# Attention: key blocks 5 and 6 of a pair added on VectorE over a strided view, two denominator groups on TensorE instead of three

## The chip, the core and the metric

The kernel runs on one core of a Trainium2 chip. The core has five engines that run side by side: TensorE (PE, matmuls into PSUM), VectorE (DVE), ScalarE (ACT), GpSimd (POOL) and SyncE (SP, which issues the transfers). Each takes its instructions in order and waits on semaphores for the others. The metric is the device time of one execution in microseconds: the kernel before has a median of 3039.39 us over 3 runs (3037.04 to 3043.93).

## The reference

One transformer block with adaptive layer norm over 4 sequences of 1024 tokens, width 1024, all in float32. Cut to what matters:

```python
x = L0_attn_x                                        # (4, 1024, 1024)
h = _layernorm(x) * (1 + ca) + sa                    # ca, sa, ga, ... from silu(c) @ wmod
q = (h @ wq_w + wq_b).reshape(bs, sl, 32, 32)        # 32 query heads
k = (h @ wk_w + wk_b).reshape(bs, sl, 8, 32)         # 8 key heads, 4 query heads on each
v = (h @ wv_w + wv_b).reshape(bs, sl, 8, 32)
attn = einsum('bqhfd,bkhd->bhfqk', qg, k) * scale    # scale 1/sqrt(32)
att = softmax(attn, axis=-1)
a = einsum('bhfqk,bkhd->bqhfd', att, v)
x = x + ga * (a @ wo_w + wo_b)
h = _layernorm(x) * (1 + cb) + sb
x = x + gb * lora_experts(h)                         # 4 experts of rank 16, the top 2 by router
```

The change concerns the softmax's denominator alone: for each head and query, the sum of exp over 1024 keys.

## The kernel before

Three stages follow one another: `project` (norm, modulation, q, k, v to DRAM), `attend`, `finish` (output projection, second norm, experts). The diff touches `attend` alone, which runs from about 690 to 2485 us of the span.

`attend` works through 64 pairs. A pair is two query heads of one key head over all 1024 queries: 4 chunks `c` of 512 queries each (`REP` = 4, `QW` = 512), and 8 key blocks of 128 keys. The keys lie in the partitions, so a tile of exponentials `p_t[:, s, c, :]` is 128 keys by 512 queries; `p_t` holds all 8 blocks of a pair, 4 x 512 words each per partition. One hardware loop covers 4 pairs a turn; the first and the last four pairs are written out.

TensorE goes through a pair in 8 steps (`do`, L999). Step s of a pair does, in this order:
- `add_num` (L951): values times exponentials of the block before, four matmuls 32 columns wide, one for each chunk, side by side in the array. In step 0 that is block 7 of the pair before.
- a denominator group, in steps 0, 1 and 3, for the pair before. A group is four matmuls of a 128x32 matrix of ones with 128x512, one for each chunk, into `den_ps`: they sum over the partitions. In steps 0 and 1 the right side is the exponentials of blocks 6 and 7 as they are (`add_den`, L965), in step 3 it is `p_sum` (`add_sum`, L977).
- in step 5 the turn of the next pair's maxima (`turn_max`, L928), which shares the bank of `den_ps`.
- `scores` (L939) of chunks 2 and 3 of block s into the two buffers of `st_ps`, then the first two chunks of the next block between the entries.
- two entries (`entry`, L912), two matmuls each: scores of a later pair, laid out with the queries in the partitions, into one of the two buffers of `s_ps`. Entry e waits until the maximum of entry e - 2 has been taken.

VectorE takes the maximum of every entry (`maximum`, L846, instruction L852), two a step, and in steps 4 to 7 the four pieces of the division for the pair before (`divide`, L862): transpose of `den_ps`, reciprocal, transpose back, product into `a_sb`. In step 6 it also makes `m_lo` (L859). ScalarE takes the exponentials (L832) and, in step 0, the copy of `num_ps`. GpSimd adds blocks 0 to 5 of a pair into `p_sum` in five additions of 128x2048 (L790), each after the exponentials of its block. ScalarE may overwrite a block of `p_t` only when all readers of it in the pair before are done (L822 to L826).

So of 8 blocks six are added by GpSimd and go to TensorE as one group, and two go there raw, one group each. SyncE loads q, k and v ahead and stores `a_sb`; the change leaves its program as it is.

Of the kernel before, what the change touches and what calls it, by code (L numbers as in the profile page):

```python
# [5 lines left out]
ALU = mybir.AluOpType  # L6
ACT = mybir.ActivationFunctionType
F32 = mybir.dt.float32
# [4 lines left out]
P = 128  # L13
# [4 lines left out]
def is_int(i, value):  # L18

    return isinstance(i, int) and i == value  # L20
# [566 lines left out]
def attend(nc, w_o, ident, wo_hi, wo_lo, q_hi_d, q_lo_d, k_hi_d, k_lo_d, v_d, att_d):  # L587
# [16 lines left out]
    ROWS = STACK + 2  # L604
    QR = 4
    NS = HEADS * NKT
    SUMMED = 6
    SUMS = SUMMED - 1
    RAWS = NKT - SUMMED
    SUM_STEP = 3  # L610
    TURN_STEP = 5
    FIRST = 18
    assert KT == NKT and NS == 16 and RAWS == 2


    START_PLAN = [(1, e) for e in range(FIRST - NS, NS)] + [(2, e) for e in range(NS // 2)]
# [3 lines left out]
    def below(i, value):  # L620
        return isinstance(i, int) and i < value
# [11 lines left out]
    with ExitStack() as ctx:  # L633
        def sb(name, shape, dt):
            return ctx.enter_context(nc.sbuf_tensor(name, shape, dt))
# [4 lines left out]
        def sem(name):  # L640
            return ctx.enter_context(nc.semaphore(name))
# [3 lines left out]
        v_sb = sb("v_sb", [P, 2, NKT, HD], F32)  # L645
        p_t = sb("p_t", [P, NKT, REP, QW], F32)
        p_sum = sb("p_sum", [P, 2, REP, QW], F32)
        ones = sb("ones", [P, HD], F32)
        mx = sb("mx", [P, 2, NS], F32)
        m_hi = sb("m_hi", [NS, P], F32R)  # L650
# [25 lines left out]
        st_ready = sem("st_ready")  # L676
        exp_done = sem("exp_done")
        num_done = sem("num_done")
        den_done = sem("den_done")
        sum_done = sem("sum_done")  # L680
        sum_used = sem("sum_used")
        num_taken = sem("num_taken")
        den_taken = sem("den_taken")
        rden_step = sem("rden_step")
# [3 lines left out]
        def pairs(eng, do):  # L688

            for pair in range(QR):  # L690
                do(pair, pair, pair // 2)
            with eng.Fori(1, NPAIR // QR - 1) as n:
                for slot in range(QR):
                    do(n * QR + slot, slot, n * 2 + slot // 2)
            for pair in range(NPAIR - QR, NPAIR):
                do(pair, pair % QR, pair // 2)

        with nc.Block() as block:
# [70 lines left out]
            @block.gpsimd  # L769
            def _(pool):  # L770
                nc.gpsimd.memset(ones[:, :], 1.0).then_inc(consts, 1)

                for k in range(KT):
                    pool.wait_ge(wo_hi_done, k + 1)
                    nc.gpsimd.tensor_tensor(wo_lo[:, k, :], p_t[:, k, 0:D // QW, :].rearrange("p j n -> p (j n)"),
                                            wo_hi[:, k, :].bitcast(F32), ALU.subtract).then_inc(wo_lo_done, 1)

                def do(pair, slot, it):
                    total = p_sum[:, slot % 2, :, :]
                    for kt in range(1, SUMMED):  # L780
                        pool.wait_ge(exp_done, pair * TILES + (kt * REP + REP))
                        if kt == 1:
                            if not below(pair, 2):

                                pool.wait_ge(sum_used, pair - 1)
                            before = p_t[:, 0, :, :]
                        else:
                            pool.wait_ge(sum_done, pair * SUMS + (kt - 1))
                            before = total
                        nc.gpsimd.tensor_tensor(total, before, p_t[:, kt, :, :], ALU.add).then_inc(sum_done, 1)  # L790

                pairs(pool, do)

            @block.scalar
            def _(act):
                for k in range(KT):
                    act.wait_ge(wo_in[k // (KT // 2)], 16)
                    nc.scalar.copy(wo_hi[:, k, :], p_t[:, k, 0:D // QW, :].rearrange("p j n -> p (j n)"))\
                      .then_inc(wo_hi_done, 1)

                def max_hi(pair):

                    act.wait_ge(m_turned, pair + 1)
                    if not is_int(pair, 0):
                        act.wait_ge(m_in, pair * 32)
                    nc.scalar.activation(m_hi[:, :], m_ps, ACT.Copy, scale=-1.0).then_inc(m_hi_done, 1)

                def take_num(pair):
                    act.wait_ge(num_done, pair * STEPS + STEPS)
                    if not below(pair, 1):  # L810

                        act.wait_ge(a_ready, pair)
                    nc.scalar.copy(num_sb[:, :], num_ps[:, :]).then_inc(num_taken, 1)

                max_hi(0)

                def do(pair, slot, it):
                    for s in range(STEPS):
                        if not below(pair, 1):


                            act.wait_ge(num_done, (pair - 1) * STEPS + (s + 1))  # L822
                            if s < SUMMED:
                                act.wait_ge(sum_done, (pair - 1) * SUMS + max(s, 1))
                            else:
                                act.wait_ge(den_done, (pair - 1) * RAWS + (s - SUMMED + 1))  # L826
                        else:

                            act.wait_ge(wo_lo_done, s + 1)
                        for c in range(REP):  # L830
                            act.wait_ge(st_ready, pair * TILES + (s * REP + c + 1))
                            nc.scalar.activation(p_t[:, s, c, :], st_ps[:, c % 2, :], ACT.Exp, scale=SCALE)\  # L832
                              .then_inc(exp_done, 1)
                            if c == 1 and s == 0 and not below(pair, 1):
                                take_num(pair - 1)
                            if c == 1 and s == TURN_STEP and not is_int(pair, NPAIR - 1):
                                max_hi(pair + 1)

                pairs(act, do)
                take_num(NPAIR - 1)  # L840

            @block.vector
            def _(dve):
# [11 lines left out]
                def max_lo(pair):  # L855
                    dve.wait_ge(m_hi_done, pair + 1)
                    if not is_int(pair, 0):
                        dve.wait_ge(m_in, pair * 32)
                    nc.vector.scalar_tensor_tensor(m_lo[:, :], m_ps, -1.0, m_hi[:, :].bitcast(F32), ALU.mult,  # L859
                                                   ALU.subtract).then_inc(m_lo_done, 1)  # L860

                def divide(pair, par, piece):  # L862


                    if piece == 0:
                        dve.wait_ge(sum_used, pair + 1)
                        nc.vector.transpose(den_t[:, :, :].rearrange("p c r -> p (c r)"), den_ps[:, :])\
                          .then_inc(den_taken, 1)
                    elif piece == 1:
# [25 lines left out]
                def do(pair, slot, it):  # L895
                    for s in range(STEPS):
                        if s == TURN_STEP + 1 and not is_int(pair, NPAIR - 1):
                            max_lo(pair + 1)
                        if s > SUM_STEP and not below(pair, 1):
                            divide(pair - 1, (slot - 1) % 2, s - SUM_STEP - 1)  # L900
                        for item in beside(pair, slot, s):
                            maximum(*item)

                pairs(dve, do)
                for piece in range(4):
                    divide(NPAIR - 1, (NPAIR - 1) % 2, piece)

            @block.tensor
            def _(pe):
# [52 lines left out]
                                                p_t[:, s, c, :], start=s == 0, stop=s == NKT - 1)  # L962
                    last.then_inc(num_done, 1)

                def add_den(pair, s):  # L965

                    if s == SUMMED:
                        if below(pair, 1):
                            pe.wait_ge(m_lo_done, 2)
                        else:  # L970
                            pe.wait_ge(a_ready, pair)
                    for c in range(REP):
                        last = nc.tensor.matmul(den_ps[c * HD:(c + 1) * HD, :], ones[:, :], p_t[:, s, c, :],
                                                start=s == SUMMED, stop=False)
                    last.then_inc(den_done, 1)

                def add_sum(pair, par):  # L977

                    pe.wait_ge(sum_done, pair * SUMS + SUMS)
                    for c in range(REP):  # L980
                        last = nc.tensor.matmul(den_ps[c * HD:(c + 1) * HD, :], ones[:, :], p_sum[:, par, c, :],
                                                start=False, stop=True)
                    last.then_inc(sum_used, 1)

                def entries(pair, part):
                    for e in part:
# [12 lines left out]
                def do(pair, slot, it):  # L999
                    for s in range(STEPS):  # L1000
# [2 lines left out]
                        before = (pair, slot, s - 1) if s else (pair - 1, (slot - 1) % QR, STEPS - 1)  # L1003
                        if not (below(pair, 1) and s == 0):
                            add_num(*before)
                        if s < RAWS and not below(pair, 1):
                            add_den(pair - 1, SUMMED + s)
                        if s == SUM_STEP and not below(pair, 1):
                            add_sum(pair - 1, (slot - 1) % 2)
                        if s == TURN_STEP and not is_int(pair, NPAIR - 1):  # L1010
                            turn_max(pair + 1, (slot + 1) % QR)

# [17 lines left out]
                    scores(0, 0, 0, c)  # L1030
                pairs(pe, do)
                add_num(NPAIR - 1, QR - 1, STEPS - 1)
                for s in range(SUMMED, NKT):
                    add_den(NPAIR - 1, s)
                add_sum(NPAIR - 1, (NPAIR - 1) % 2)


def finish(nc, x, b_o, lora_in, lora_out, earlier_in, ident, wo_hi, wo_lo, att_d, mod_raw_d, mod_gate_d, out):
# [504 lines left out]
```

## Time and profile before

| | before |
|---|---|
| median of 3 runs | 3039.39 us |
| lowest, highest | 3037.04, 3043.93 us |
| profiled execution, its own time | 3039.35 us |
| its span, first to last instruction | 3037.6 us |
| TensorE busy in the span | 2899.8 us (95%) |
| VectorE busy | 1930.1 us (64%) |
| GpSimd busy | 1799.0 us (59%) |
| ScalarE busy | 1525.5 us (50%) |
| mean granted clock of TensorE | 0.975 |

A busy share over the whole span averages three stages with different limits, so it has to be read by stage. Within a stage the timeline tells more than the sums: it gives the start of each instruction, and what ended the idle time before it in brackets. Matmuls are pipelined: the next starts before the last has ended, so the distance between two starts is the price of one, not its duration. The same holds on VectorE for instructions that wait for nothing. Of two merged instructions ("x2") the row gives the start of the first and the time to the end of the last.

### The profile page before, as it was taken

How to read it: one execution, taken by the hardware profiler on the slowest of the kernel's cores; microseconds unless marked ns; L12 is line 12 of the kernel's file. 1: busy time of each engine (PE TensorE's matmuls, PEld its weight loads, DVE VectorE, ACT ScalarE, POOL GpSimd, SP SyncE). 2: the span in 40 equal slices, each digit the busy share in tenths (PEclk: the TensorE clock that was granted, in tenths of full speed). 3: DMA queues.
4: the chain of work that ended last, by engine and by line, in shares of the span. 5: the costliest groups of instructions: out<-in, count | busy, mean ns of one | idle time of the engine just before them, and what ended most of it. 6: DMA issues, size and time to landing. Idle time of an engine off the chain costs nothing. (4 is left out here: it accounts for less than half of the span.)

```text
span 3037.6 us, 49792 instructions
## 1 busy us (share of the span) xinstructions
PE 2899.8 (95%) x15590; PEld 1743.7 (57%) x15590; DVE 1930.1 (64%) x2572; ACT 1525.5 (50%) x2906; POOL 1799.0 (59%) x595
## 2 busy tenths in 40 slices
PE   6899999989999999999999999999999978999997
PEld 3687878864444444444444444444444427777776
DVE  3333333327777777777777777777777717666666
ACT  2211111115666666666666666666666643444444
POOL 2433333317888888888888888888888865111110
PEclk7899999988999999999999999999999989999998
DMA  6543333341222122212211221122122123322331
GB/s 228 171 139 131 132 132 132 120 149 41 55 52 53 38 51 55 48 39 54 51 43 47 51 55 39 47 55 51 36 54 51 29 83 109 105 92 95 104 104 63
DMA packets 156463, 241.61 MB, mean 80 GB/s; under 512 B 48993, under 2 KB 90401, under 8 KB 156321
## 3 DMA queue, kind: packets, MB, share of 16 engines
q1 hardware_dynamic: 156320, 240.05, 27.3%
q8 instruction: 48, 0.79, 0.1%
q14 instruction: 95, 0.77, 0.1%
HBM read 159.12 MB, written 79.82 MB: 79 GB/s over the span
## 5 line engine op out<-in xcount | busy, mean ns | idle before, releaser
L852 DVE TENSOR_REDUCE mx<-s_ps 128x1 f32<-128x1024 f32 x1024 | 1203.5, 1216 | 430.3 <-PE s_ps L921 424.4
L832 ACT ACTIVATE p_t<-st_ps 128x512 f32<-128x512 f32 x2048 | 1112.6, 595 | 552.9 <-PE st_ps L947 483.9
L790 POOL TENSOR_TENSOR p_sum<-p_sum,p_t 128x2048 f32<-128x2048 f32 x256 | 1173.8, 4585 | 22.1
L947 PE MATMUL st_ps<-q_st,k_st 98*128 98x512 f32 x2048 | 811.2, 436 | 10.7 <-ACT p_t L832 7.7
L947 PEld LDWEIGHTS st_ps<-q_st,k_st 98*128 98x128 f32 x2048 | 345.1, 187 | 604.8 <-ACT p_t L832 414.2
L921 PE MATMUL s_ps<-k_st,q_st 96*128 96x512 f32 x2048 | 655.9, 402 | 14.5 <-DMA q_st<-q_hi_d 10.8
L961 PE MATMUL num_ps<-p_t,v_sb 128*32 128x512 f32 x4096 | 546.4, 605 | 0.9 <-ACT p_t L832 0.9
L790 POOL TENSOR_TENSOR p_sum<-p_t 128x2048 f32<-128x2048 f32 x64 | 293.3, 4584 | 293.8 <-ACT p_t L832 293.8
L921 PEld LDWEIGHTS s_ps<-k_st,q_st 96*128 96x128 f32 x2048 | 389.6, 191 | 93.7 <-DVE mx L852 14.1
L372 POOL TENSOR_TENSOR o_lo<-side,o_hi 128x512 fp32r<-128x512 f32 x80 | 104.6, 1308 | 345.1 <-ACT o_hi L342 345.1
L1231 POOL TENSOR_TENSOR a_lo<-a_f,a_hi 128x1024 fp32r<-128x1024 f32 x32 | 76.2, 2380 | 390.3 <-ACT a_hi L1266 390.2
L557 PE MATMUL o_ps<-h_hi,w_hi 128*128 128x512 f32 x608 | 243.1, 400 | 2.5 <-issue 2.4
L557 PE MATMUL o_ps<-h_hi,w_lo 128*128 128x512 f32 x608 | 239.6, 394 | 0.0
L557 PE MATMUL o_ps<-h_lo,w_hi 128*128 128x512 f32 x608 | 239.4, 394 | 0.0
L461 DVE TENSOR_SCALAR side<-o_ps,bias_qk 128x512 f32<-128x512 f32 x80 | 59.9, 749 | 277.5 <-PE o_ps L557 275.0
L342 ACT CAST o_hi<-side 128x512 fp32r<-128x512 f32 x80 | 49.7, 621 | 356.0 <-DVE side L461 344.6
L1425 PE MATMUL o_ps<-wo_hi,a_hi 128*128 128x512 f32 x512 | 205.9, 402 | 13.8 <-POOL a_lo L1231 13.8
L1425 PE MATMUL o_ps<-wo_lo,a_hi 128*128 128x512 f32 x512 | 205.2, 401 | 0.0
L1425 PE MATMUL o_ps<-wo_hi,a_lo 128*128 128x512 f32 x512 | 205.0, 400 | 0.0
L1282 ACT ACTIVATE h_t<-t_ps,shift,scale 128x128 f32<-128x128 f32 x256 | 92.8, 468 | 195.0 <-PE t_ps L1488 195.0
L961 PEld LDWEIGHTS num_ps<-p_t,v_sb 128*32 128x32 f32 x4096 | 80.6, 108 | 129.5 <-issue 125.6
L363 POOL TENSOR_TENSOR h_lo<-h_f,h_hi 128x256 fp32r<-128x256 f32 x128 | 91.6, 737 | 100.7 <-ACT h_hi L335 100.7
(129 smaller groups left out, 2819.3 us busy)
## 6 DMA issues: line engine op xcount, KB each, us to landing
q_st<-q_hi_d SPq DMA_DIRECT2D x128, 256.0 KB, 4.5
stage<-w_mod SPq DMA_DIRECT2D x48, 512.0 KB, 5.7
q_hi_d<-o_hi SPq DMA_DIRECT2D x64, 256.0 KB, 2.0
q_lo_d<-o_lo SPq DMA_DIRECT2D x64, 256.0 KB, 2.0
q_st<-q_lo_d SPq DMA_DIRECT2D x64, 256.0 KB, 4.1
att_d<-a_sb SPq DMA_DIRECT2D x128, 128.0 KB, 2.3
a_f<-att_d SPq DMA_DIRECT2D x32, 512.0 KB, 4.7
x_sb<-x SPq DMA_DIRECT2D x32, 512.0 KB, 5.3
```

The lines of the kernel that those rows point to most:

```text
L363: nc.gpsimd.tensor_tensor(h_lo[:, 1 - par, kt, cols], h_f[:, bank_at(i, hf, kt), :], h_hi[:, 1 - par, kt, cols].bitcast(F32), ALU.subtract)\
L372: nc.gpsimd.tensor_tensor(o_lo[:, g % 2, :], o_f[:, g % 2, :], o_hi[:, g % 2, :].bitcast(F32), ALU.subtract)\
L557: last = nc.tensor.matmul(o_ps[:, bank, :], w[:, kt, g * P:(g + 1) * P], h[:, par, kt, :], start=begin, stop=end)
L790: nc.gpsimd.tensor_tensor(total, before, p_t[:, kt, :, :], ALU.add).then_inc(sum_done, 1)
L832: nc.scalar.activation(p_t[:, s, c, :], st_ps[:, c % 2, :], ACT.Exp, scale=SCALE)\
L852: nc.vector.tensor_reduce(mx[:, slot % 2, e:e + 1], s_ps[:, e % 2, :], AX_X, ALU.max)\
L921: part = nc.tensor.matmul(s_ps[:, e % 2, n * QW:(n + 1) * QW], q_st[0:STACK, slot, jj, t * P:(t + 1) * P], k_st[0:STACK, slot // 2, n * QW ...
L947: nc.tensor.matmul(st_ps[:, c % 2, :], k_st[:, slot // 2, s * P:(s + 1) * P], q_st[:, slot, jj, h * QW:(h + 1) * QW], start=True, stop=True)\
L961: last = nc.tensor.matmul(num_ps[c * HD:(c + 1) * HD, :], v_sb[:, slot // 2, s, :], p_t[:, s, c, :], start=s == 0, stop=s == NKT - 1)
L1231: nc.gpsimd.tensor_tensor(a_lo[:, u, :, :], a_f[:, u, :, :], a_hi[:, u, :, :].bitcast(F32), ALU.subtract).then_inc(a_lo_done, 1)
L1282: last = nc.scalar.activation(h_t[:, tt % 2, kt, :], t_ps[:, kt * P:(kt + 1) * P], ACT.Identity, bias=batch(shift2, bb)[:, kt:kt + 1], sca ...
L1425: last = nc.tensor.matmul(o_ps[:, u, cols], a[:, u, k, :], w[:, k, cols], start=(k == 0 and n == 0), stop=(k == KT - 1 and n == 2))
```

## The change

GpSimd now adds blocks 0 to 4 and 7 (`ADDED`), again in five additions; the last one follows the exponentials of block 7. Blocks 5 and 6 are added by VectorE: for each chunk c one `tensor_reduce` with add over `p_t[:, 5:7, c, :]`, seen with the block as the innermost dimension, so that every output is the sum of two words that lie 4 x 512 words (8 KB) apart in the partition. It writes 512 words of a new buffer `two_sum`. Chunk 0 is done in step 7 of the pair itself, chunks 1 to 3 in steps 0, 1 and 2 of the next, each time ahead of that step's two maxima. TensorE now has two denominator groups a pair: over `p_sum` in step 2 and over `two_sum` in step 3; `add_den` is gone. ScalarE waits for the last reduction before it overwrites blocks 5 and 6.

```diff
-    SUMMED = 6
-    SUMS = SUMMED - 1
-    RAWS = NKT - SUMMED
-    SUM_STEP = 3
+    ADDED = (0, 1, 2, 3, 4, 7)
+    SUMS = len(ADDED) - 1
+    TWO = 5
+    SUM_STEP = 2
+    TWO_STEP = 3
...
+        two_sum = sb("two_sum", [P, REP, QW], F32)
...
-                            if s < SUMMED:
-                                act.wait_ge(sum_done, (pair - 1) * SUMS + max(s, 1))
+                            if s in ADDED:
+                                act.wait_ge(sum_done, (pair - 1) * SUMS + max(ADDED.index(s), 1))
                             else:
-                                act.wait_ge(den_done, (pair - 1) * RAWS + (s - SUMMED + 1))
+                                act.wait_ge(two_done, (pair - 1) * REP + REP)
...
+                def add_two(pair, c):
+
+                    dve.wait_ge(exp_done, pair * TILES + ((TWO + 1) * REP + c + 1))
+                    if c == 0 and not below(pair, 1):
+                        dve.wait_ge(two_used, pair)
+                    nc.vector.tensor_reduce(two_sum[:, c, :], p_t[:, TWO:TWO + 2, c, :].rearrange("p s q -> p q s"),
+                                            AX_X, ALU.add).then_inc(two_done, 1)
...
-                        if s > SUM_STEP and not below(pair, 1):
-                            divide(pair - 1, (slot - 1) % 2, s - SUM_STEP - 1)
+                        if s > TWO_STEP and not below(pair, 1):
+                            divide(pair - 1, (slot - 1) % 2, s - TWO_STEP - 1)
+                        if s < REP - 1 and not below(pair, 1):
+                            add_two(pair - 1, s + 1)
+                        if s == STEPS - 1:
+                            add_two(pair, 0)
                         for item in beside(pair, slot, s):
                             maximum(*item)
...
+                def add_two(pair):
+
+                    pe.wait_ge(two_done, pair * REP + REP)
+                    for c in range(REP):
+                        last = nc.tensor.matmul(den_ps[c * HD:(c + 1) * HD, :], ones[:, :], two_sum[:, c, :],
                                                 start=False, stop=True)
-                    last.then_inc(sum_used, 1)
+                    last.then_inc(two_used, 1)
...
-                        if s < RAWS and not below(pair, 1):
-                            add_den(pair - 1, SUMMED + s)
                         if s == SUM_STEP and not below(pair, 1):
                             add_sum(pair - 1, (slot - 1) % 2)
+                        if s == TWO_STEP and not below(pair, 1):
+                            add_two(pair - 1)
```

The queue of VectorE before, where pair 2 ends and pair 3 begins: from the maxima of step 6 and the product `a_sb` of step 7 to the division of step 4 and 5 (`mx` are the maxima, `den_t` and `rden_c` pieces of the division).

```order
L852 TENSOR_REDUCE mx<-s_ps 128x1 x2
L885 TENSOR_TENSOR a_sb<-den_ps,num_sb 128x512
L852 TENSOR_REDUCE mx<-s_ps 128x1 x10
L867 STREAM_TRANSPOSE den_t<-den_ps 128x512
L852 TENSOR_REDUCE mx<-s_ps 128x1 x2
L871 RECIPROCAL rden_c<-den_t 128x16
```

The same place now: from the maxima of step 6 of pair 2 to the transpose in step 4 of pair 3 (`two_sum<-p_t` is the new reduction).

```order
L855 TENSOR_REDUCE mx<-s_ps 128x1 x2
L896 TENSOR_TENSOR a_sb<-den_ps,num_sb 128x512
L870 TENSOR_REDUCE two_sum<-p_t 128x512
L855 TENSOR_REDUCE mx<-s_ps 128x1 x2
L870 TENSOR_REDUCE two_sum<-p_t 128x512
L855 TENSOR_REDUCE mx<-s_ps 128x1 x2
L870 TENSOR_REDUCE two_sum<-p_t 128x512
L855 TENSOR_REDUCE mx<-s_ps 128x1 x2
L870 TENSOR_REDUCE two_sum<-p_t 128x512
L855 TENSOR_REDUCE mx<-s_ps 128x1 x4
L878 STREAM_TRANSPOSE den_t<-den_ps 128x512
```

The ten maxima in a row between `a_sb` and `den_t` now have four reductions among them, one ahead of each of the first four steps' maxima (steps 7, 0, 1, 2).

The queue of TensorE before, steps 0 and 1 of pair 3 (`num_ps` are the values, `den_ps` the denominator, `st_ps` and `s_ps` the two kinds of scores).

```order
L961 MATMUL num_ps<-p_t,v_sb 32x512 x4
L973 MATMUL den_ps<-p_t,ones 32x512 x4
L947 MATMUL st_ps<-q_st,k_st 128x512 x2
L921 MATMUL s_ps<-k_st,q_st 128x512 x3
L947 MATMUL st_ps<-q_st,k_st 128x512
L921 MATMUL s_ps<-k_st,q_st 128x512
L947 MATMUL st_ps<-q_st,k_st 128x512
L961 MATMUL num_ps<-p_t,v_sb 32x512 x4
L973 MATMUL den_ps<-p_t,ones 32x512 x4
L947 MATMUL st_ps<-q_st,k_st 128x512 x2
```

TensorE now, from step 1 of pair 3 to the start of step 2.

```order
L978 MATMUL num_ps<-p_t,v_sb 32x512 x4
L964 MATMUL st_ps<-q_st,k_st 128x512 x2
L938 MATMUL s_ps<-k_st,q_st 128x512 x3
L964 MATMUL st_ps<-q_st,k_st 128x512
L938 MATMUL s_ps<-k_st,q_st 128x512
L964 MATMUL st_ps<-q_st,k_st 128x512
L978 MATMUL num_ps<-p_t,v_sb 32x512 x4
L990 MATMUL den_ps<-p_sum,ones 32x512 x4
L964 MATMUL st_ps<-q_st,k_st 128x512 x2
```

Step 1 has no denominator group any more (nor has step 0), and step 2 has the one over `p_sum`; the one over `two_sum` follows in step 3.

## Rows read from the trace of the kernel before

**Rows 1.** Page, part 2: busy tenths in 40 slices of the span.
```profile
PE   6899999989999999999999999999999978999997
...
DVE  3333333327777777777777777777777717666666
```

**Rows 2.** Busy time in one stretch: PE, PEld, DVE, ACT, POOL, clock, DMA.
```profile
1400.00:2400.00 1000.00, 998.79 (x5555) 469.40 (x5557) 757.10 (x758) 656.15 (x1228) 826.03 (x181) 1.00 0.20 48
```

**Rows 3.** Timeline, TensorE: start us, us, engine, line, what, count.
```profile
1502.34 1.07 PE L961 MATMUL num_ps<-p_t,v_sb 128*32 128x512 f32 x8
...
1503.34 0.73 PE L947 MATMUL st_ps<-q_st,k_st 98*128 98x512 f32 x2
...
1506.43 0.72 PE L947 MATMUL st_ps<-q_st,k_st 98*128 98x512 f32 x2
...
1508.60 1.07 PE L961 MATMUL num_ps<-p_t,v_sb 128*32 128x512 f32 x8
...
1510.45 0.73 PE L947 MATMUL st_ps<-q_st,k_st 98*128 98x512 f32 x2
...
1514.41 0.73 PE L947 MATMUL st_ps<-q_st,k_st 98*128 98x512 f32 x2
...
1517.50 0.72 PE L947 MATMUL st_ps<-q_st,k_st 98*128 98x512 f32 x2
...
1518.07 0.85 PE L921 MATMUL s_ps<-k_st,q_st 96*128 96x512 f32 x3
...
1518.75 0.43 PE L947 MATMUL st_ps<-q_st,k_st 98*128 98x512 f32 x1
...
1529.95 0.64 PE L961 MATMUL num_ps<-p_t,v_sb 128*32 128x512 f32 x4
```

**Rows 4.** One line's instructions, L806: durations ns, first and last start us.
```profile
L806 ACT ACTIVATE m_hi<-den_ps x64: 266/267/268, 692.7 to 2442.7; 16x128 fp32r<-16x128 f32 x64
```

**Rows 5.** Timeline, VectorE, same stretch.
```profile
1504.76 2.32 DVE L852 TENSOR_REDUCE mx<-s_ps 128x1 f32<-128x1024 f32 x2
1507.00 0.67 DVE L885 TENSOR_TENSOR a_sb<-den_ps,num_sb 128x512 f32<-128x512 f32 x1
1507.66 2.36 DVE L852 TENSOR_REDUCE mx<-s_ps 128x1 f32<-128x1024 f32 x2
...
1518.72 2.36 DVE L852 TENSOR_REDUCE mx<-s_ps 128x1 f32<-128x1024 f32 x2 [0.72 <-PE s_ps L921]
```

**Rows 6.** Groups of instructions: busy us, mean ns, idle us before them.
```profile
L852 DVE TENSOR_REDUCE mx<-s_ps 128x1 f32<-128x1024 f32 x1024 | 1203.5, 1216 | 430.3 <-PE s_ps L921 424.4
L790 POOL TENSOR_TENSOR p_sum<-p_sum,p_t 128x2048 f32<-128x2048 f32 x256 | 1173.8, 4585 | 22.1
```

**Rows 7.** Timeline of pair 0, VectorE and TensorE.
```profile
711.34 3.49 DVE L852 TENSOR_REDUCE mx<-s_ps 128x1 f32<-128x1024 f32 x3 [0.67 <-PE s_ps L921]
...
711.63 0.39 PE L921 MATMUL s_ps<-k_st,q_st 96*128 96x512 f32 x1
...
712.62 0.73 PE L921 MATMUL s_ps<-k_st,q_st 96*128 96x512 f32 x2 [0.33 <-DVE mx L852]
```

**Rows 8.** Groups of VectorE, shapes apart: copies, reductions, a two-input operation.
```profile
L1324 DVE TENSOR_TENSOR x<-x,x_sb 128x1024 f32<-128x1024 f32 x32 | 41.4, 1293 | 1.1
...
L1381 DVE TENSOR_REDUCE rank<-above 128x4 f32<-128x16 f32 x32 | 5.4, 169 | 1.1
...
L1389 DVE TENSOR_REDUCE total<-wts 128x1 f32<-128x4 f32 x32 | 5.0, 157 | 1.1
...
L1305 DVE COPY shift<-t_ps 128x32 f32<-128x32 f32 x1 | 0.2, 192 | 16.3 <-PE t_ps L1458 16.3
...
L429 DVE COPY shift<-t_ps 128x32 f32<-128x32 f32 x1 | 0.2, 191 | 1.2 <-PE t_ps L531 1.2
```

**Rows 9.** Timeline, end of the last pair.
```profile
2472.50 9.23 POOL L790 TENSOR_TENSOR p_sum<-p_sum,p_t 128x2048 f32<-128x2048 f32 x2
...
2481.78 1.06 PE L981 MATMUL den_ps<-p_sum,ones 128*32 128x512 f32 x8 [1.16 <-POOL p_sum L790]
```

More of the change, by code:

```diff
@@ L606, in attend @@
     NS = HEADS * NKT
-    SUMMED = 6
-    SUMS = SUMMED - 1
-    RAWS = NKT - SUMMED
-    SUM_STEP = 3
+    ADDED = (0, 1, 2, 3, 4, 7)
[3 more added lines that the diff above has]
+    TWO_STEP = 3
     TURN_STEP = 5
     FIRST = 18
-    assert KT == NKT and NS == 16 and RAWS == 2
+    assert KT == NKT and NS == 16 and sorted(ADDED + (TWO, TWO + 1)) == list(range(NKT))
     START_PLAN = [(1, e) for e in range(FIRST - NS, NS)] + [(2, e) for e in range(NS // 2)]
@@ L678, in attend @@
         num_done = sem("num_done")
-        den_done = sem("den_done")
         sum_done = sem("sum_done")
         sum_used = sem("sum_used")
+        two_done = sem("two_done")
+        two_used = sem("two_used")
         num_taken = sem("num_taken")
@@ L779, in do @@
                     total = p_sum[:, slot % 2, :, :]
-                    for kt in range(1, SUMMED):
+                    for n, kt in enumerate(ADDED[1:]):
                         pool.wait_ge(exp_done, pair * TILES + (kt * REP + REP))
-                        if kt == 1:
+                        if n == 0:
                             if not below(pair, 2):
                                 pool.wait_ge(sum_used, pair - 1)
-                            before = p_t[:, 0, :, :]
+                            before = p_t[:, ADDED[0], :, :]
                         else:
-                            pool.wait_ge(sum_done, pair * SUMS + (kt - 1))
+                            pool.wait_ge(sum_done, pair * SUMS + n)
                             before = total
@@ L860, in max_lo @@
                                                    ALU.subtract).then_inc(m_lo_done, 1)
+                def add_two(pair, c):
[4 more added lines that the diff above has]
+                                            AX_X, ALU.add).then_inc(two_done, 1)
                 def divide(pair, par, piece):
                     if piece == 0:
-                        dve.wait_ge(sum_used, pair + 1)
+                        dve.wait_ge(two_used, pair + 1)
                         nc.vector.transpose(den_t[:, :, :].rearrange("p c r -> p (c r)"), den_ps[:, :])\
@@ L904, in _ @@
                 pairs(dve, do)
+                for c in range(1, REP):
+                    add_two(NPAIR - 1, c)
                 for piece in range(4):
@@ L963, in add_num @@
                     last.then_inc(num_done, 1)
[L965 to L975, printed above, removed]
                 def add_sum(pair, par):
                     pe.wait_ge(sum_done, pair * SUMS + SUMS)
+                    if below(pair, 1):
+                        pe.wait_ge(m_lo_done, 2)
+                    else:
+                        pe.wait_ge(a_ready, pair)
                     for c in range(REP):
                         last = nc.tensor.matmul(den_ps[c * HD:(c + 1) * HD, :], ones[:, :], p_sum[:, par, c, :],
+                                                start=True, stop=False)
+                    last.then_inc(sum_used, 1)
+                def add_two(pair):
+                    pe.wait_ge(two_done, pair * REP + REP)
+                    for c in range(REP):
+                        last = nc.tensor.matmul(den_ps[c * HD:(c + 1) * HD, :], ones[:, :], two_sum[:, c, :],
                                                 start=False, stop=True)
-                    last.then_inc(sum_used, 1)
+                    last.then_inc(two_used, 1)
                 def entries(pair, part):
@@ L1032, in _ @@
                 add_num(NPAIR - 1, QR - 1, STEPS - 1)
-                for s in range(SUMMED, NKT):
-                    add_den(NPAIR - 1, s)
                 add_sum(NPAIR - 1, (NPAIR - 1) % 2)
+                add_two(NPAIR - 1)
 def finish(nc, x, b_o, lora_in, lora_out, earlier_in, ident, wo_hi, wo_lo, att_d, mod_raw_d, mod_gate_d, out):
```

## The prediction

> **What bounds the kernel now.** I read the page's slices first: the middle of the run, from about 690 to 2440 us, has TensorE at nine tenths or more of every slice, VectorE at seven [rows 1]. The summed stretch of that middle says it exactly: TensorE is busy 998.79 of 1000 us at a granted clock of 1.00, VectorE 757, GpSimd 826 [rows 2]. The change lies only in this attention stage, so I then read the stage as a sequence. Blocks below are the eight key blocks of a pair, steps the eight passes of the loop in `do`, and the start of a step is taken where its first pair of `st_ps` matmuls starts.
>
> An ordinary step takes 3.10 us: 1503.34 to 1506.43 [rows 3]. A step with a denominator group takes 3.96 (1510.45 to 1514.41). A whole pair takes 27.61 us (1502.34 to 1529.95 for the same `num_ps` group) and the mean over the 63 distances between 64 pairs is (2442.7 - 692.7) / 63 = 27.78 [rows 3, 4]; the difference is the turn of the hardware loop every fourth pair. TensorE never waits in there, so anything taken from its queue is time, as long as nobody else becomes late.
>
> Who could is VectorE. Its 16 maxima a pair read `s_ps`, which has two buffers. In the step that starts at 1517.50 the first entry matmul starts 0.57 later; three entries are 1518.75 - 1518.07 = 0.68 us, so 0.23 each, and the third starts 1.03 after the step's start. The first maximum starts at 1518.72, 1.22 after it, and two take 2.36 [rows 3, 5]. With 1.22 for one [rows 6], the second starts 1.14 behind the first. The third entry of a step may start when the second maximum of the step before has ended. The handover is seen where it does bind: three maxima from 711.34 end the first at 712.56, and TensorE's entry starts at 712.62, 0.06 later; its two matmuls then take 0.73, where two at the usual spacing take 0.23 + 0.39 = 0.62, so a broken stream costs 0.11 more [rows 6, 7]. I call the distance from a step's start to its first maximum the lag. TensorE waits when lag + 2.36 + 0.06 is over step + 1.03, for an ordinary step when the lag is over 1.71. The largest lag now is 1.42, in step 6 (1504.76 - 1503.34), and 1.23 in step 7 [rows 3, 5]. Nothing waits.
>
> **The change, part by part.** Removed from TensorE: one of three denominator groups a pair. Its price is 3.96 - 3.10 = 0.86 us, and 64 of them are 55 us. The other two groups move from steps 0, 1 and 3 to steps 2 and 3; the order of the queue shows this, and their cost is unchanged.
>
> Added to VectorE: four reductions a pair, each 128x1024 in and 128x512 out, ahead of the two maxima in steps 7, 0, 1 and 2. No row shows such an operation. The nearest rows: the maximum over as many elements, from PSUM, has 1.22 and a spacing of 1.14 [rows 5, 6]. Writing more outputs seems free: a reduction of 16 to 4 takes 169 ns, one of 4 to 1 takes 157, so 12 more elements read and three more written are 12 ns [rows 8]. The far view is the open point, since neighbours in the inner direction lie 8 KB apart. The only pair of rows on a far step is a copy of 32 elements out of PSUM with a step of 8 elements, 191 ns, and one without a step, 192 ns [rows 8]: no price there, though it is PSUM and short. Bounds: from below 0.67 us, a 128x512 operation (`a_sb`, 1507.00 to 1507.66) [rows 5], if only outputs counted; from above 2.28, twice the spacing of the maximum, if every hop cost one more element's time; the two-input operation of 1024 elements in SBUF, 1.29 [rows 8], lies between. I take 1.14, the row of the same operation and size.
>
> One rule speaks against this. The Trainium skill, "Vector Engine (DVE) Microarchitecture Reference", section 5.2, says that a port streams at full rate only over runs of two adjacent words, and gives 1.73 ns per column for one source that hops at every element. By it a reduction has some 1.8 us, an estimate from that page. The same section adds that a one-source operation whose stream alternates between two regions 16 KiB apart, writing one word for two read, ran at the full rate, which is nearly this view. No row here shows either; the sum goes by the maximum's row, and the slow one is a rival.
>
> Now the chain. After step 6 VectorE no longer has idle time. From the start of step 6: its first maximum 1.42 later. To that of step 7: two maxima 2.28, the product `a_sb` 0.66 and one reduction 1.14, together 4.08, where the step has 3.10: the lag becomes 2.4, over 1.71, and TensorE waits in step 0. To the first maximum of step 0: 2.28 + 1.14 = 3.42. The third entry of step 1 waits for that step's second maximum: 2.36 + 0.06. From there to the next step 3.10 - 1.03 = 2.07, with 0.11 for the restart, and the group now in step 2, 0.86. Sum from step 6 to step 2: 1.42 + 4.08 + 3.42 + 2.42 + 2.07 + 0.11 + 0.86 = 14.38 us. Before it is 1517.50 - 1503.34 = 14.16 [rows 3]. So the pair does not get shorter by 0.86; it gets 0.22 longer. The waits in steps 0 and 1 take about 1.1 us. In step 2 the long step lets VectorE catch up: the third entry is free 0.4 after its start and due at 1.03. Steps 3 to 6 are as before.
>
> 63 distances by 0.22 are +14 us. Against it: the loop's turn, 27.78 - 27.61 = 0.17 a pair, partly falls into the wait in step 0 since the chain there is VectorE's; I give it half, -5. In the last pair there is no entry to wait for; its sums end on GpSimd, at 2481.73, and TensorE waited for them [rows 9]. Two groups fewer stand ahead of its first sum (-1.7), and one more group stands behind the last (+0.9): -0.8. Sum: +8 us on the profiled execution's own 3039.35, 3047. That execution stands at the median of 3039.39, so nothing is to be corrected.
>
> What I cost at nothing. GpSimd's fifth sum is now over block 7 and not 5. The `num_ps` group of that block starts at 1508.60, so its exponentials are done by then [rows 3]; 4.59 later [rows 6] is 1513.2. Step 2 starts at 1517.50 now, its `num_ps` group 1.00 before; less the two groups that went ahead of it and plus that `num_ps` group's 0.86, its denominator group comes at 1516.5 - 1.7 + 0.9 = 1515.7 at the earliest: 2.5 us to spare. GpSimd has 5 x 4.59 = 22.9 us a pair of 27. ScalarE's wait for blocks 5 and 6 is for reductions made three steps earlier. TensorE's group over `two_sum` follows the last reduction by more than a microsecond. If the first cover went, each us would be 63.
>
> **Rivals.** First, the hop is paid. Place: the same chain, one or two steps longer. For a spacing y it is 15.80 + 4y from step 6 to step 4 (1.42 + 2.94 + 3 x 2.28 + 4y + 2.42 + 2.07 + 0.11), against 14.16 + 3.96 + 3.10 = 21.22 before. At 2.28 that is 24.9, +3.7 a pair, some 3270 us; the load of VectorE itself, 0.757 x 27.6 + 4 x 2.28 = 30.0 a pair, is over 27.6 as well. Halfway, at 1.71, it is 22.6, +1.4 and some 3128. For it: no row has two neighbours so far apart. Against it: the copy with a step. By the Trainium skill's 1.73 ns per column (same page and section), an estimate, the sum would be some 3155.
>
> Second, on the other side: faster. The two reductions in the chain (steps 7 and 0) decide twice: from step 6 to 2 the chain is 12.10 + 2y, equal to 14.16 at y = 1.03. Below that TensorE's group comes back. At the lower bound of 0.67 the chain gives 13.44, 0.72 less a pair, 2993 us. At 0.95, or if the handover is looser than 0.06 and the restart is not paid, 3026 to 3034. For it: a result only every second element. Against: 1.14 for the same count of inputs.
>
> Third, the change does nothing to the order of the work: excluded by the queues, which have the reductions and one group less.
>
> **How the numbers follow.** Forecast 0.64: 3047, own range 3034 to 3062, from 0.1 us either way on the spacing (two reductions, 63 pairs: 13 us). The hop paid 0.19, the cheaper chain 0.17. The range goes down to 3026 and up to 3165, which leaves out the doubled reduction and the cheapest. A change of 0.2%, 6 us, is about what a measurement of this kernel can tell from none. Within the forecast: slower 0.39, same 0.23, faster 0.02; with the rivals (0.19 slower; 0.15 faster and 0.02 same) slower 0.58, same 0.25, faster 0.17.
>
> **What would show it.** The reduction's mean duration near 1.2 us; VectorE without idle time from step 6 to step 2; TensorE's entries idle on `mx`, about 1 us a pair in two steps, where there is none now; steps 3 to 6 unchanged at 3.10 and 3.96; TensorE's busy share of the stage down from 99.9% to about 97% at clock 1.00; a pair of 27.8 us. Wrong it would be with a reduction of 1.8 us or more, or of 1.0 or less, or with a wait of TensorE on `p_sum`.

## The result, and the profile after

| | before | after |
|---|---|---|
| median | 3038.52 us (20 runs) | 3044.82 us (20 runs) |
| lowest, highest | 3030.67, 3045.82 | 3040.46, 3050.40 |
| profiled execution | 3039.35 us | 3043.16 us |

The ratio of the runs is 1.0022, with a 95% interval of 1.0013 to 1.0031: 4 to 9 us slower. Forecast was 8 us slower. A denominator group of TensorE is gone from each of 64 pairs, and the kernel is no faster.

The page's slices show first where it went: VectorE, at seven tenths before [rows 1], is at nine.

```profile
PE   6899999989999999999999999999999968999997
...
DVE  3333333328999999999998999999899937666666
```

In the same stretch as [rows 2], TensorE is busy 979.33 us where it had 998.79, at the same clock of 1.00, and VectorE 909.53 where it had 757.10. TensorE has less to do and about 2% of idle time.

```profile
1400.00:2400.00 1000.00, 979.33 (x5252) 458.03 (x5244) 909.53 (x899) 650.82 (x1224) 823.13 (x181) 1.00 0.20 48
```

The new group of VectorE, with busy time, mean and idle time: 1240 ns a reduction, 24 more than the 1216 of a maximum before [rows 6].

```profile
L855 DVE TENSOR_REDUCE mx<-s_ps 128x1 f32<-128x1024 f32 x1024 | 1200.4, 1212 | 167.2 <-PE s_ps L938 159.3
...
L870 DVE TENSOR_REDUCE two_sum<-p_t 128x512 f32<-128x1024 f32 x256 | 316.9, 1240 | 6.2 <-ACT p_t L835 6.2
```

Waits from 800 to 2400 us: in total, times, the longest. There was none of these in the steady state before.

```profile
PEld s_ps L938 <- DVE mx L855: 58.4, 90, 0.8
...
PE s_ps L938 <- DVE mx L855: 15.9, 44, 0.4
```

The timeline of TensorE, to be read against [rows 3]. A pair takes 1528.56 - 1500.87 = 27.69 us, where it took 27.61. An entry is two matmuls here, and the "third entry" of a step is the third of its four entry matmuls, the first that needs the second maximum of the step before. The bracket at 1509.68 is the wait for that maximum, at the third entry of step 0.

```profile
1500.87 1.06 PE L978 MATMUL num_ps<-p_t,v_sb 128*32 128x512 f32 x8
...
1501.87 0.73 PE L964 MATMUL st_ps<-q_st,k_st 98*128 98x512 f32 x2
...
1504.96 0.73 PE L964 MATMUL st_ps<-q_st,k_st 98*128 98x512 f32 x2
...
1508.12 0.73 PE L964 MATMUL st_ps<-q_st,k_st 98*128 98x512 f32 x2
...
1509.68 0.50 PE L938 MATMUL s_ps<-k_st,q_st 96*128 96x512 f32 x1 [0.38 <-DVE mx L855]
...
1511.80 0.73 PE L964 MATMUL st_ps<-q_st,k_st 98*128 98x512 f32 x2
...
1516.10 0.74 PE L964 MATMUL st_ps<-q_st,k_st 98*128 98x512 f32 x2
...
1528.56 1.06 PE L978 MATMUL num_ps<-p_t,v_sb 128*32 128x512 f32 x8
```

VectorE in the same stretch, to be read against [rows 5]. From the maxima of step 6 (1503.29) to the last reduction (1516.39) it has no idle time.

```profile
1503.29 2.32 DVE L855 TENSOR_REDUCE mx<-s_ps 128x1 f32<-128x1024 f32 x2
1505.53 0.68 DVE L896 TENSOR_TENSOR a_sb<-den_ps,num_sb 128x512 f32<-128x512 f32 x1
1506.12 1.24 DVE L870 TENSOR_REDUCE two_sum<-p_t 128x512 f32<-128x1024 f32 x1
1507.28 2.34 DVE L855 TENSOR_REDUCE mx<-s_ps 128x1 f32<-128x1024 f32 x2
1509.55 1.24 DVE L870 TENSOR_REDUCE two_sum<-p_t 128x512 f32<-128x1024 f32 x1
1510.70 2.34 DVE L855 TENSOR_REDUCE mx<-s_ps 128x1 f32<-128x1024 f32 x2
1512.97 1.24 DVE L870 TENSOR_REDUCE two_sum<-p_t 128x512 f32<-128x1024 f32 x1
1514.13 2.33 DVE L855 TENSOR_REDUCE mx<-s_ps 128x1 f32<-128x1024 f32 x2
1516.39 1.25 DVE L870 TENSOR_REDUCE two_sum<-p_t 128x512 f32<-128x1024 f32 x1
```

The lag is 1503.29 - 1501.87 = 1.42 in step 6 (forecast 1.42), 1507.28 - 1504.96 = 2.32 in step 7 (forecast 2.4), and the first maximum of step 0 follows 3.42 later, at 1510.70 (forecast 3.42). The third entry of step 0 starts at 1509.68: two maxima end at 1507.28 + 2.34 = 1509.62, and the handover is 0.06. From step 6 to step 2 it is 1516.10 - 1501.87 = 14.23 us, where it was 14.16 and 14.38 was forecast. Step 0 takes 1511.80 - 1508.12 = 3.68 us and step 1 4.30; without waits, in experiment 4, they take 3.18 and 3.97. So the waits take 0.83 us a pair, where about 1.1 was forecast.

Over all pairs, by the line of `m_hi` as in [rows 4]: (2445.0 - 691.1) / 63 = 27.84 where it was 27.78.

```profile
L809 ACT ACTIVATE m_hi<-den_ps x64: 266/266/268, 691.1 to 2445.0; 16x128 fp32r<-16x128 f32 x64
```

### The profile page after: what moved, and what is told of

The parts are those of the page before. It is cut to its first block and busy times, and to the rows that moved or that the text cites. A ratio compares the mean times of both kernels' runs of the same rounds, so it can differ in the third digit from the quotient of the medians.

```text
span 3041.4 us, 49431 instructions
## 1 busy us (share of the span) xinstructions
PE 2867.3 (94%) x15078; PEld 1723.5 (57%) x15078; DVE 2207.6 (73%) x2828; ACT 1520.6 (50%) x2906; POOL 1797.6 (59%) x595
## 5 line engine op out<-in xcount | busy, mean ns | idle before, releaser
L938 PE MATMUL s_ps<-k_st,q_st 96*128 96x512 f32 x2048 | 682.1, 407 | 36.7 <-DVE mx L855 21.2
L870 DVE TENSOR_REDUCE two_sum<-p_t 128x512 f32<-128x1024 f32 x256 | 316.9, 1240 | 6.2 <-ACT p_t L835 6.2
```

What stands on the lines that cost most here:

```text
L870: nc.vector.tensor_reduce(two_sum[:, c, :], p_t[:, TWO:TWO + 2, c, :].rearrange("p s q -> p q s"), AX_X, ALU.add).then_inc(two_done, 1)
L938: part = nc.tensor.matmul(s_ps[:, e % 2, n * QW:(n + 1) * QW], q_st[0:STACK, slot, jj, t * P:(t + 1) * P], k_st[0:STACK, slot // 2, n * QW ...
```

## The experiments

Each kernel ran beside the kernel before on the same chip. Ratios are to it, with the 95% interval.

**1. No reductions.** The waits for them stay, as plain increments:

```diff
-                    nc.vector.tensor_reduce(two_sum[:, c, :], p_t[:, TWO:TWO + 2, c, :].rearrange("p s q -> p q s"),
-                                            AX_X, ALU.add).then_inc(two_done, 1)
+                    dve.sem_inc(two_done, 1)
```

> The changed kernel without VectorE's reductions: `two_sum` is filled with ones once, so the sums of blocks 5 and 6 are left out. Theory A (the removed denominator group is worth its 0.86 us a pair, and late maxima behind the reductions take it back): no wait of TensorE on mx, 64 x 0.86 = 55 us less than before, some 2984 us. Theory B (the group was worth less, because TensorE's step has another limit): clearly above 3000 us.

Measured: 3009.32 us against 3042.12, ratio 0.9887 (0.9865 to 0.9908), 33 us less. From 800 to 2400 us of its trace TensorE's entries wait for a maximum once, 0.3 us. So the reductions take back what the group gives, but the group gives 33 and not 55. Theory A is right on who, and too high on how much. The time is above 3000, as theory B had it, and B is right that a step of TensorE has another limit in places: experiment 4 shows that it is ScalarE.

**2. The reductions alone,** in the kernel before, at the same places, with its three groups:

```diff
+                        if s < REP - 1 and not below(pair, 1):
+                            add_two(pair - 1, s + 1)
+                        if s == STEPS - 1:
+                            add_two(pair, 0)
```

> The kernel before with the four reductions a pair added at the places of the change, and the three denominator groups left as they were, in steps 0, 1 and 3; the reductions' result is not used. Theory A: the long steps 0 and 1 of before leave room. Lag 2.3 in step 7 against a limit of 2.6 ahead of a step of 4.02, 1.7 in step 0 against 2.6, 1.2 in step 1, 1.6 in step 2: no wait, within 3 us of before. Theory C (the reductions cost by themselves: reads that slow other engines, or VectorE's load): 3045 us or more, and longer additions of GpSimd or exponentials.

Measured: 3039.71 us against 3042.12, ratio 0.9996 (0.9984 to 1.0008). 256 reductions of 1.24 us cost nothing where the steps are long, and no entry waits for a maximum from 800 to 2400 us. GpSimd's addition takes 4585 ns as before [rows 6] and an exponential 595. That excludes contention and the bare load as a cause (theory C).

**3. Without the reduction in step 7,** and its counterpart **5, without the one in step 2.** Both take one of four from VectorE:

```diff
+                    if c == 0:
+                        dve.sem_inc(two_done, 1)
+                        return
```

(with `c == 3` in experiment 5).

> The changed kernel without the reduction of chunk 0, the one in step 7; its part of `two_sum` is ones, so blocks 5 and 6 are left out for that chunk. Theory A: the lag is 1.2 in step 7, 1.5 in step 0 and 1.8 in step 1, under the limits of 1.7, 1.7 and 2.6: no wait at all, some 2985 us, as without any reduction. Theory C (what counts is VectorE's load): a quarter of the difference between all four and none, some 3030 us.

> The changed kernel without the reduction of chunk 3, the one in step 2; its part of `two_sum` is ones. The counterpart to dropping the one in step 7: the same load is taken off VectorE. Theory A: step 2's reduction lies behind the last entry that waits, so nothing changes, 3044 us. Theory C (load): some 3030 us, as for any one of the four.

Measured: without the one in step 7, 3002.94 us, ratio 0.9871 (0.9852 to 0.9889). Without the one in step 2, 3045.90 us, ratio 1.0019 (1.0004 to 1.0033), as slow as with all four. The waits for a maximum, from 800 to 2400 us, first without step 7's, then without step 2's:

```profile
PEld s_ps L942 <- DVE mx L856: 0.5, 2, 0.3
```

```profile
PEld s_ps L942 <- DVE mx L856: 59.6, 92, 0.8
...
PE s_ps L942 <- DVE mx L856: 16.3, 45, 0.4
```

The first is 0.5 us in two waits, the second the same 59.6 as with all four (58.4). The same load taken off, all of the price in one case and none in the other: what counts is the chain from step 6 to the third entry of step 1, not VectorE's busy share. The first time lies 18 us above the 2985 that was expected, for the reason that experiment 4 shows.

**4. Each reduction one step later,** in steps 0 to 3, and TensorE's group over `two_sum`, which has to follow the last of them, ahead of the `num_ps` group of step 4:

```diff
-                        if s < REP - 1 and not below(pair, 1):
-                            add_two(pair - 1, s + 1)
-                        if s == STEPS - 1:
-                            add_two(pair, 0)
+                        if s < REP and not below(pair, 1):
+                            add_two(pair - 1, s)
...
+                        if s == TWO_STEP + 1 and not below(pair, 1):
+                            add_two(pair - 1)
                         if not (below(pair, 1) and s == 0):
                             add_num(*before)
```

> All four reductions, each one step later (steps 0, 1, 2, 3), and TensorE's group over two_sum behind step 3 instead of in it, ahead of the num_ps group of step 4. The same work on every engine. Theory A: lags of 1.2, 1.5, 1.8, 1.3 and 1.6 in steps 7 to 3, none over its limit (1.7, 1.7, 2.6, 1.7, 2.6): some 2985 us, 1.8% under before. Theory C (load or contention): no change against the changed kernel, 3044 us.

Measured: 3005.33 us against 3042.12, ratio 0.9876 (0.9859 to 0.9894): the same instructions on every engine, and 1.2% faster than before, where the changed kernel is 0.2% slower. It beats both kernels. It lies 20 us above the expected 2985, and its trace tells why. The starts of `m_hi`, one a pair:

```profile
1024.32 0.27 ACT L809 ACTIVATE m_hi<-den_ps 16x128 fp32r<-16x128 f32 x1 [0.68 <-PE den_ps L951]
...
1052.39 0.27 ACT L809 ACTIVATE m_hi<-den_ps 16x128 fp32r<-16x128 f32 x1 [0.68 <-PE den_ps L951]
...
1079.23 0.27 ACT L809 ACTIVATE m_hi<-den_ps 16x128 fp32r<-16x128 f32 x1 [0.68 <-PE den_ps L951]
...
1106.08 0.27 ACT L809 ACTIVATE m_hi<-den_ps 16x128 fp32r<-16x128 f32 x1 [0.68 <-PE den_ps L951]
```

The first distance is a pair behind a turn of the hardware loop, 28.07 us; the other two are 26.84 and 26.85. Before, the same were 28.06 and 27.62 (from its trace). So the missing group gives 0.77 in an ordinary pair and nothing in each fourth; over all 13 pairs behind a turn the mean is 28.12 before and 28.13 here. Without waits the pair is the same in experiments 1 and 3: 26.85.

The 0.77 instead of 0.86: step 0 takes 1090.59 - 1087.40 = 3.19 without a group, not 3.10. ScalarE copies `num_ps` in it, between the exponentials (timeline):

```profile
1087.40 1.07 PE L976 MATMUL num_ps<-p_t,v_sb 128*32 128x512 f32 x8
...
1088.53 0.58 ACT L816 COPY num_sb<-num_ps 128x512 f32<-128x512 f32 x1 [0.42 <-PE num_ps L976]
...
1090.59 1.06 PE L976 MATMUL num_ps<-p_t,v_sb 128*32 128x512 f32 x8
```

The nothing: ScalarE comes late behind its branch. At a turn its first exponential starts 1.39 after the `num_ps` group, and TensorE waits for it with its scores until 1469.44:

```profile
1467.40 1.06 PE L976 MATMUL num_ps<-p_t,v_sb 128*32 128x512 f32 x8
...
1468.79 1.08 ACT L835 ACTIVATE p_t<-st_ps 128x512 f32<-128x512 f32 x2 [1.93 <-PE num_ps L976]
...
1469.44 0.98 PE L962 MATMUL st_ps<-q_st,k_st 98*128 98x512 f32 x2 [0.97 <-ACT p_t L835]
```

The bracket names `num_ps`, but the exponential does not use that group: at the turn shown in experiment 8 the same exponential starts 2.4 us ahead of it, after a pause of 2.27 us. In the kernel before, the same pause is there, 2.17 us of ScalarE, and a denominator group stood in it:

```profile
1480.27 1.07 PE L961 MATMUL num_ps<-p_t,v_sb 128*32 128x512 f32 x8
...
1481.15 1.04 PE L973 MATMUL den_ps<-p_t,ones 128*32 128x512 f32 x8
...
1481.90 1.08 ACT L832 ACTIVATE p_t<-st_ps 128x512 f32<-128x512 f32 x2 [2.17 <-PE num_ps L961]
```

The loop's 14 passes have 13 such turns. So 13 of 64 groups had been hidden all along; 51 x 0.77 = 39 us is what the group was worth, and 37 were measured.

**6. The view.** The same 1024 words in and 512 out, of adjacent words:

```diff
-                    nc.vector.tensor_reduce(two_sum[:, c, :], p_t[:, TWO:TWO + 2, c, :].rearrange("p s q -> p q s"),
+                    nc.vector.tensor_reduce(two_sum[:, c, :], p_t[:, TWO + c // 2, c % 2 * 2:c % 2 * 2 + 2, :]
+                                            .rearrange("p c (q w) -> p (c q) w", w=2),
```

> The changed kernel with the reductions over adjacent words: each adds neighbouring queries of block 5 or 6, the same 1024 words in and 512 out, so the blocks' sums are mixed up among queries. If the view over 8 KB costs nothing: the same 1.24 us and 3044 us. If it costs part of the 25 ns that the reduction has over the maximum: 1.21 us, and 3041 us.

Measured: 1206 ns, 34 less than over the far view, and 3044.80 us against 3040.62, ratio 1.0019 (1.0008 to 1.0029). The far view costs 34 ns of 1240. The duration came out as in the second case expected, the time as in the first. In the trace an ordinary pair takes 27.60 us, 0.08 less than with the far view (27.68), as two reductions in the chain would have it; those 5 us do not show between the two ratios, 1.0019 and 1.0022.

```profile
L870 DVE TENSOR_REDUCE two_sum<-p_t 128x512 f32<-128x1024 f32 x256 | 308.2, 1206 | 6.2 <-ACT p_t L835 6.2
```

**7. Hops that reach no neighbour,** queries 16 apart and the two blocks innermost:

```diff
+                    nc.vector.tensor_reduce(junk[:, c % 2, :].rearrange("p (b a) -> p b a", b=16),
+                                            p_t[:, TWO:TWO + 2, c, :].rearrange("p s (a b) -> p b a s", b=16),
+                                            AX_X, ALU.add).then_inc(two_done, 1)
```

> The changed kernel with the reduction's view walked so that both streams jump: queries 0, 16, 32 and so on, the two blocks innermost, so that no two reads in 32 fall on neighbouring words; written to a spare buffer, with two_sum left at ones. Theory D (full rate comes from the two alternating streams each walking adjacent words): the reduction gets slower, 1.7 to 2.6 us, as by the section on the access granule in the Trainium skill's page Vector Engine (DVE) Microarchitecture Reference, and the kernel 3130 to 3330 us. Theory E (a hop is free for a one-input operation): 1.24 us and 3044 us.

Measured: 2025 ns, and 3168.78 us against 3040.62, ratio 1.0422 (1.0404 to 1.0439). Theory D holds.

```profile
L874 DVE TENSOR_REDUCE junk<-p_t 128x512 f32<-128x1024 f32 x256 | 518.0, 2025 | 6.2 <-ACT p_t L836 6.2
```

A pair takes 1110.07 - 1080.32 = 29.75 us:

```profile
1080.32 0.27 ACT L810 ACTIVATE m_hi<-den_ps 16x128 fp32r<-16x128 f32 x1 [0.68 <-PE den_ps L958]
...
1110.07 0.27 ACT L810 ACTIVATE m_hi<-den_ps 16x128 fp32r<-16x128 f32 x1 [0.67 <-PE den_ps L958]
```

The prediction's chain for this rival, 15.80 + 4y at a spacing of 2025 less the 0.08 by which a follower starts early, y = 1.94, gives 23.56, 2.34 over the 21.22 of before, a pair of 29.95. That rival was well priced; its condition did not arise.

**8, 9 and 10. The turn of the loop.** The later placement with 8 and with 28 pairs in a turn, and the kernel before with 8:

```diff
-            with eng.Fori(1, NPAIR // QR - 1) as n:
-                for slot in range(QR):
-                    do(n * QR + slot, slot, n * 2 + slot // 2)
+            with eng.Fori(0, (NPAIR - 2 * QR) // 8) as n:
+                for j in range(8):
+                    do(n * 8 + (QR + j), j % QR, n * 4 + (QR + j) // 2)
```

> The later placement with 8 pairs in a turn of the hardware loop instead of 4: 7 turns, not 14, nothing else changed. A pair behind a turn takes 28.1 us there against 26.85, since ScalarE has its first exponentials about 2 us late after its branch. Theory A (that is why the removed group gave 0.77 us in an ordinary pair and nothing at a turn): 7 x 1.2 = 8 us under the 3005 of the later placement, some 2997 us. Theory F (the cost lies in loading code, by length and not by turn): no gain, 3005 us or more.

> The kernel before with 8 pairs in a turn of the loop. Its pair behind a turn takes 28.1 against 27.62, since the denominator group of step 0 runs in ScalarE's pause. Theory A: 7 x 0.45 = 3 us under before, 3037 us. Theory F: no gain or slower.

> The later placement with 28 pairs in a turn: 2 turns instead of 14. Theory A: 12 x 1.2 = 15 us under the 3005 of the later placement, some 2990 us, near the 55 us of 64 groups. Theory F: longer straight code brings the same pauses elsewhere, 3000 us or more.

Measured: 3033.59 us, ratio 0.9977 (0.9966 to 0.9989), where 4 pairs in a turn gave 0.9876; the kernel before 3073.71, ratio 1.0112 (1.0095 to 1.0130); 28 pairs 3001.48, ratio 0.9877 (0.9857 to 0.9898). My expectations of 2997, 3037 and 2990 were all too low, and theory F is nearer. Where the loop of 8 no longer turns, the cost is gone: the pairs half way through its body take 26.85, so it belongs to the turn and not to every fourth pair. But a turn of 8 pairs is dearer than two of 4: a pair behind it takes 1047.53 - 1012.95 = 34.58 us, and the six turns 32.1 to 35.2, 33.7 in the mean. The one turn of the 28-pair loop costs as much, 33.44, so from 8 pairs on the price did not grow with the body.

```profile
1012.95 0.27 ACT L809 ACTIVATE m_hi<-den_ps 16x128 fp32r<-16x128 f32 x1 [0.68 <-PE den_ps L951]
...
1047.53 0.27 ACT L809 ACTIVATE m_hi<-den_ps 16x128 fp32r<-16x128 f32 x1 [0.68 <-PE den_ps L951]
```

At that turn ScalarE pauses 2.27 and TensorE 4.10 us; `issue` means that the profile shows nothing that they waited for. TensorE's group then takes 1.93, where it has 1.07: it comes back at a granted clock of 0.50, the 1.2 GHz level (second fence).

```profile
1022.87 1.08 ACT L835 ACTIVATE p_t<-st_ps 128x512 f32<-128x512 f32 x2 [2.27 <-issue]
...
1025.30 1.93 PE L976 MATMUL num_ps<-p_t,v_sb 128*32 128x512 f32 x8 [4.10 <-issue]
```

```profile
1025.30:1030.00 4.70, 4.70 (x15) 2.46 (x16) 1.09 (x2) 1.67 (x3) 0.00 (x0) 0.50 0.81 203
```

The instruction queue of the page (packets, MB) carries 121 packets with 8 pairs and 47 with 4 (119 with 28, and 137 in the kernel before with 8):

```profile
q8 instruction: 121, 1.98, 0.3%
```

```profile
q8 instruction: 47, 0.77, 0.1%
```

Longer loop bodies are fetched anew on each turn, it seems: the packets and the pauses are shown, the reason (no room to hold the body) is argued. With 28 pairs the loop branches back once, and 3001 against 3005 us of the 4-pair loop is within their intervals: whether one dear turn is better than 13 cheap ones stays open. In the two traces the time from the first to the last `m_hi` is 1703.3 us with 28 pairs and 1712.1 with 4, but that is one execution each.

## Why the prediction was right, step by step

- **The bound.** TensorE without waits, VectorE the one to become late: right, and experiments 3 and 5 show it most sharply. The limit of 1.71 on the lag fits: a lag of 1.52 ahead of an ordinary step (step 0 in experiment 4) brings no wait, one of 2.32 does.
- **The reduction's spacing.** Taken as 1.14 from the maximum's row; the trace has 1510.70 - 1509.55 = 1.15. The duration, forecast near 1.2, is 1.24. The choice against the slow view was right, and section 5.2 of the Trainium skill's page "Vector Engine (DVE) Microarchitecture Reference" is borne out on both sides: its bracketed case, one stream between two far regions, here 8 KB apart, took 1240 ns, near the 1206 over adjacent words, and a view close to its hop at every element took 2025, somewhat over the 1.8 us that was estimated from its 1.73 ns per column.
- **The chain.** Forecast 14.38 from step 6 to step 2, measured 14.23. 0.09 is in step 7: 3.99 for the 4.08 between the two first maxima, since the reduction follows the product after 0.59 and not 0.66 and the product follows the maxima after 2.24 and not 2.28, against 0.02 more for the reduction. 0.02 is the end of the second maximum (2.34 for 2.36), and 0.04 the restart. With 0.07 instead of 0.22 a pair this term is +4 us and not +14.
- **The loop's turn.** Half of its 0.17 a pair was to fall into the wait, -5 us. The pair behind the same turn took 28.06 before and 28.04 after (its `m_hi` at 1026.44 and 1054.48), so the same, and only the 0.07 falls away there: at most -1 over 13 turns. One of the 13 took 29.81 after, 1.7 more than the others; TensorE ran at a granted clock of 0.78 for 7.6 us there, and the kernel without reductions has such a turn too (29.74), so it is not put down to the reductions. With it this term is about +1. I had not seen that the turn is ScalarE's pause, in which the removed group stood; had the chain not bound, the first term, 55 us, would have been too high by half: 37 were measured in experiment 4.
- **The end.** Forecast -0.8, measured some +2.5: from the last `m_hi` to the product `a_sb` it is 2489.49 - 2445.0 = 44.5, and was 2484.7 - 2442.7 = 42.0. Two things missed. GpSimd's last addition now waits for block 7, and starts at 2479.42; it ends 38.9 us after the last `m_hi`, where it ended 39.0 after it before, so the -1.7 did not come. And the two groups behind it run at half the clock, 1.7 from one to the next, after TensorE had been idle for 3.5 us; before, the one group there took 1.06 after 1.2 us of idle time. From the first group to the transpose it is 3.7 us, where it was 1.1.

```profile
2479.42 4.51 POOL L793 TENSOR_TENSOR p_sum<-p_sum,p_t 128x2048 f32<-128x2048 f32 x1 [1.65 <-ACT p_t L835]
...
2483.98 1.94 PE L990 MATMUL den_ps<-p_sum,ones 128*32 128x512 f32 x8 [3.52 <-POOL p_sum L793]
...
2485.69 1.94 PE L998 MATMUL den_ps<-two_sum,ones 128*32 128x512 f32 x8
...
2487.69 0.72 DVE L878 STREAM_TRANSPOSE den_t<-den_ps 128x512 f32<-128x512 f32 x1 [9.02 <-PE den_ps L998]
```

The stretch's granted clock is 0.50, the 1.2 GHz level:

```profile
2484.00:2490.00 6.00, 3.62 (x16) 0.58 (x16) 2.21 (x4) 0.00 (x0) 0.00 (x0) 0.50 0.00 0
```

- **Sum.** Forecast +8, measured +3.8 in the profiled execution and +6.3 in the medians, interval 4 to 9. The sizes of three terms were off by 10, 4 to 6 and 3 us, in different directions; the mechanism was as described. That the sum came within 4 us is in part luck, since the second and third errors cancelled most of the first. In the profiled execution 3.9 us lie between the first and the last `m_hi` (3.0 in the 48 ordinary pairs, 2.0 in the 13 behind a turn, -1.1 in the first two), 2.5 in the end of the stage, -1.6 ahead of the first (691.1 for 692.7) and about -1 behind the stage; the last two belong to no term.
- **The covers.** GpSimd's fifth sum is never waited for in the steady state, as said; ScalarE's wait for blocks 5 and 6 neither.

## What to carry to other kernels

Ask of work moved to an engine with idle time not how much idle time it has, but in which steps, and how many buffers stand between it and the engine that feeds it: with two buffers, two reductions of 1.15 us in the wrong steps cost all that a removed 0.86 gave, and the same four, one step later, cost nothing that these runs can tell. Price a removed instruction in each of the places where it stands: one that stood in another engine's pause is worth nothing there. And unrolling a hardware loop further can make its turn dearer.

## What the runs showed of the hardware

- A VectorE reduction over two streams 8 KB apart is within 34 ns of one over a single stream if each stream walks adjacent words (1240 ns for 1024 words, 1206 over adjacent ones); with 16 words between the steps of each stream it takes 2025.
- Four reductions a pair beside GpSimd's additions and ScalarE's exponentials changed neither (4585 and 595 ns in the second experiment).
- A loop turn of 4 pairs costs ScalarE a pause of some 2 us, and the pair behind it takes 28.1 us for 26.85. At one of 8 pairs TensorE stood still for 4.10 us, and the pair behind it took 34.58; the mean of the six is 33.7.
